# Channel mixing in 64-row products: one product per batch in place of one per pair of batches

## The reference, cut to what matters

```
agg_w = jnp.einsum('bk,koi->boi', att, weight[..., 0])
agg_b = att @ bias_k
y = jnp.einsum('boi,bih->boh', agg_w, x) + agg_b[:, :, None]
logits = y_flat @ W_router.T          # top 2 of 8, softmax over both
h = jnp.einsum('nd,erd->ner', y_flat, A)
expert_out = jnp.einsum('ner,eor->no', h * combine[:, :, None], B) * 2
out = x + y_flat @ W_base.T + b_base + expert_out
```

## Time and profile before

| what | value |
|---|---|
| device time, median of 3 runs | 1076.33 us (1075.97 to 1076.43) |
| span of the profiled execution | 1074.3 us |
| outside this span, up to the median | 2.0 us |
| instructions | 16995 |
| TensorE busy (matmul records) | 97% of the span |
| VectorE, ScalarE, GpSimd busy | 51%, 19%, 19% |

### The profile page before, as it was taken

One profiled execution on the slowest core, in us unless ns is written; L12 is line 12 of the kernel. 1 busy time (PEld: TensorE's weight loads), 2 busy tenths in 40 slices (PEclk: granted clock), 3 DMA queues, 4 the chain that ended last, 5 costly groups with the idle time before them and its releaser, 6 DMA issues.

```text
span 1074.3 us, 16995 instructions
## 1 busy us (share of the span) xinstructions
PE 1043.5 (97%) x6289; PEld 1037.5 (97%) x6289; DVE 543.5 (51%) x1298; ACT 201.2 (19%) x404; POOL 206.8 (19%) x138
## 2 busy tenths in 40 slices
PE   2799999999999999999999999999999999999998
PEld 1799999999999999999999999999999999999998
DVE  5854554554554554554554554554554554554551
ACT  5311211211211211211211211211211211211210
POOL 4621211211211211211211211211211211211210
PEclk9999999999999999999999999999999999999999
DMA  6621221221221221221221221221221221221200
GB/s 189 235 86 46 83 85 45 83 85 45 83 85 45 83 85 45 83 85 45 83 85 45 83 85 45 83 83 48 83 85 46 82 85 46 82 85 46 83 40 40
DMA packets 41836, 82.43 MB, mean 77 GB/s; under 512 B 13626, under 2 KB 24890, under 8 KB 41658
## 3 DMA queue, kind: packets, MB, share of 16 engines
q1 hardware_dynamic: 41826, 82.30, 23.9%
HBM read 46.46 MB, written 35.68 MB: 76 GB/s over the span
## 4 chain that ended last, share of the span: by engine, by line
PE 96%; DVE 2%; issue 1%; DMA 1%; ACT 0%; SPq 0%; DVEq 0%
PE ps_main L337 25%; PE ps_main L336 25%; PE ps_main L338 25%; PE ps_main L345 8%; PE ps_y L329 6%; PE ps_y L328 6%; DMA mix_space<-in_mix_w 1%; PE ps_main L409 1%; DVE y_parts L235 0%; PE ps_main L350 0%; DVE y_parts L579 0%; DMA mix<-mix_space 0%; DVE y_sb L569 0%; DVE mix_parts L558 0%; DVE y_sb L565 0%
## 5 line engine op out<-in xcount | busy, mean ns | idle before, releaser
L336 PE MATMUL ps_main<-w_hi,y_parts 128*128 128x388 f32 (+1 forms) x1536 | 526.0, 342 | 0.0
L337 PE MATMUL ps_main<-w_lo,y_parts 128*128 128x388 f32 (+1 forms) x1536 | 521.2, 339 | 0.0
L338 PE MATMUL ps_main<-w_hi,y_parts 128*128 128x388 f32 (+1 forms) x1536 | 520.1, 339 | 0.0
L336 PEld LDWEIGHTS ps_main<-w_hi,y_parts 128*128 128x128 f32 x1536 | 289.3, 188 | 2.3
L337 PEld LDWEIGHTS ps_main<-w_lo,y_parts 128*128 128x128 f32 x1536 | 289.7, 189 | 0.0
L338 PEld LDWEIGHTS ps_main<-w_hi,y_parts 128*128 128x128 f32 x1536 | 289.2, 188 | 0.0
L514 POOL TENSOR_TENSOR x_sb<-x_sb,bias_out 128x1024 f32<-128x1024 f32 x64 | 153.5, 2398 | 252.4 <-DVE x_lo L553 252.4
L436 ACT CAST y_parts<-y_sb 128x512 fp32r<-128x512 f32 x128 | 79.3, 620 | 378.6 <-DVE y_sb L569 378.6
L328 PE MATMUL ps_y<-mix_parts,x_hi 128*128 128x256 f32 x508 | 127.7, 283 | 10.9 <-DVE mix_parts L558 5.8
L510 POOL TENSOR_TENSOR mix_parts<-mix,mix_parts 128x128 fp32r<-128x128 f32 x62 | 28.7, 463 | 559.0 <-ACT mix_parts L432 559.0
L574 DVE TENSOR_TENSOR y_parts<-y_sb,y_parts 128x512 fp32r<-128x512 f32 x128 | 88.6, 692 | 87.8 <-ACT y_parts L436 87.7
(11 more groups left out here) (68 smaller groups left out, 470.3 us busy)
## 6 DMA issues: line engine op xcount, KB each, us to landing
x_sb<-in_x SPq DMA_DIRECT2D x64, 512.0 KB, 4.0
result<-x_sb SPq DMA_DIRECT2D x64, 512.0 KB, 2.7
bias_y<-agg_b_rows SPq DMA_DIRECT2D x64, 64.0 KB, 3.2
w_stage<-in_wide SPq DMA_DIRECT2D x4, 776.0 KB, 6.9
agg_w_rows<-mix_space SPq DMA_DIRECT2D x1, 2048.0 KB, 11.1
mix<-agg_w_rows SPq DMA_DIRECT2D x120, 16.0 KB, 2.2
w_stage<-in_wide SPq DMA_DIRECT2D x2, 768.0 KB, 11.6
mix_space<-in_mix_w SPq DMA_DIRECT2D x1, 650.0 KB
```

Source lines behind the costliest of these rows:

```text
L336: nc.tensor.matmul(dst, y_hi[:, u, cols], w_hi[:, c, piece], start=c == 0, stop=False)
L337: nc.tensor.matmul(dst, y_hi[:, u, cols], w_lo[:, c, piece], start=False, stop=False)
L338: return nc.tensor.matmul(dst, y_lo[:, u, cols], w_hi[:, c, piece], start=False, stop=c == DC - 1)
```

## The change

Each product over 128 stationary rows becomes two over 64 rows, one for each batch `b` of the pair. Rows 0 to 63 of `x_hi` meet the 64 columns of the first batch in the high part and the 64 in the low part of `mix_parts`, 128 moving columns in all; rows 64 to 127 meet those of the second batch. A call now issues 16 products with 16 weight loads. The products of the two batches are issued in turn (high part: batch 0, batch 1; low part: batch 0, batch 1). `ps_y` is laid out anew so that each batch has one of the two banks, and the two sums on VectorE read it in runs of 64 columns. Nothing else is changed; blank lines at the top of the file are gone, so that line numbers move by 16.

```
-        ps_y = ctx.enter_context(nc.psum_tensor("ps_y", [P, HC, 2, P], F32))
-        ps_y_flat = ps_y[:].rearrange("p c k n -> p (c k n)")
-        ps_y_first = ps_main[:, 1, 1:3, :].rearrange("p h (c k n) -> p (h c) k n", k=2, n=P)
+        ps_y = ctx.enter_context(nc.psum_tensor("ps_y", [P, PAIR, HC, 2, CH], F32))
+        ps_y_flat = ps_y[:].rearrange("p b c k o -> p (b c k o)")
+        ps_y_first = ps_main[:, 1, 1:3, :].rearrange("p b (c k o) -> p b c k o", k=2, o=CH)
...
                 for j in range(HC):
                     cols = slice((g * HC + j) * P, (g * HC + j + 1) * P)
-                    dst = into[:, j, :, :].rearrange("p k n -> p (k n)")
-                    nc.tensor.matmul(dst, x_hi[:, u, cols], mix_parts[:, u, :], start=True, stop=False)
-                    mm = nc.tensor.matmul(dst, x_lo[:, u, cols], mix_parts[:, u, :], start=False, stop=True)
+                    for part, first in ((x_hi, True), (x_lo, False)):
+                        for b in range(PAIR):
+                            rows = slice(b * CH, (b + 1) * CH)
+                            dst = into[:, b, j, :, :].rearrange("p k o -> p (k o)")
+                            own = mix_parts[rows, u, :].rearrange("p (k n) -> p k n", k=2)[:, :, rows]
+                            mm = nc.tensor.matmul(dst, part[rows, u, cols], own, start=first, stop=not first)
                 mm.then_inc(y_mm, 1)
...
             def y_sum(t, s, g, from_=ps_y):
 
-                half = y_sb[:, g * HD:(g + 1) * HD].rearrange("p (c n) -> p c n", c=HC)
+                half = y_sb[:, g * HD:(g + 1) * HD].rearrange("p (c b o) -> p c b o", c=HC, b=PAIR)
+                high, low = (from_[:, :, :, k, :].rearrange("p b c o -> p c b o") for k in range(2))
+                bias = bias_y[:, s, :].rearrange("p (b o) -> p b o", b=PAIR).unsqueeze(1)
                 dve.wait_ge(y_mm, halves(t, g))
-                nc.vector.tensor_tensor(half, from_[:, :, 0, :],
-                                        bias_y[:, s, :].unsqueeze(1).to_broadcast([P, HC, P]),
+                nc.vector.tensor_tensor(half, high, bias.to_broadcast([P, HC, PAIR, CH]),
                                         ALU.add).then_inc(y_part, 1)
                 dve.wait_ge(y_part, halves(t, g))
-                nc.vector.tensor_tensor(half, from_[:, :, 1, :], half, ALU.add).then_inc(y_summed, 1)
+                nc.vector.tensor_tensor(half, low, half, ALU.add).then_inc(y_summed, 1)
```

## The result

The changed kernel takes 1111.2 us (median of 4 runs, 1111.12 to 1111.36) against 1076.15 us: a ratio of 1.0326, 95% interval 1.0312 to 1.0341. It is slower by 35 us. I had forecast 1179 us. The measured time is close to that of the second rival (1110 us).

The account below looks back on a forecast made before the run. TensorE, busy 1043.5 of 1074.3 us, was taken as the bound; 125 calls at +0.81 us (+101) and the third call's +1.7 made +103 on 1076.3, so 1179 us, with row changes, sums and banks at nothing; range 1064 to 1212.

Parts of the forecast that it names:

- the second rival: Mixing on TensorE: both halves' loads side by side, but each 128/64-row change stops the array 0.17 us; 1110 us, chance 0.21.
- part (1): Mixing call: 16 loads one after another at 0.110 us, 1.76 us in place of 0.95; +101 us over 125 calls.
- the rule against the rows: Skill's rule that different tiles load and multiply in parallel, against traced load order; by it a small gain.
- the first rival: Mixing on TensorE: halves' loads side by side, row changes free; 0.88 us a call, -9 us, 1067 us, chance 0.27.
- Part (3): Array changing between 128 and 64 rows, 250 times on the path: forecast nothing; 0.17 us each, +43 us, for the range.
- Part (4): Two VectorE sums reading PSUM in runs of 64 columns, 0.68 and 0.69 us now: covered, cost 0.
- Part (5): PSUM banks of `ps_y`: two banks kept, each written until a call's end, nothing else reads them meanwhile; cost 0.
- part (2): Count of 128 mixing calls: first two hidden at start-up, third on the path +1.7 us, other 125 pay fully.

Follow-up runs that it names:

- the last run: Kernel before the change, low part of x multiplied by the mixing matrix's high part alone, 128 columns for 256 in every second product: 1073.1 us, ratio 0.9973.

## Why the prediction was wrong

The step that failed is part (1), "if the loads follow one another, each at the start of the product ahead as in the earlier trace rows". I read an order that holds for the same 128 rows as the order of all loads. In the changed kernel the second half's load starts within 0.01 us of the first's, ahead of a product that is still waiting. The section on the rule against the rows named this point: the Trainium skill (TensorEngine Tiling (Array Packing), Key Properties) says that tiles load and multiply in parallel, and here the traces agree, with 0.11 us for a pair of loads as for one. So a call costs 8 steps of a load and not 16: in place of the forecast's +101 us for part (1) the runs have -6 us (0.05 us in each of 125 calls). I weighted an observation that could not tell the cases apart over a rule that did.

The size of a load was right: 0.107 to 0.11 us for 128 float32r columns from the earlier trace rows, and the runs show 0.11 us in 64 rows and in 128. The run over all rows gave 1180.7 us where this price gives 1179. Because of it, the first rival's limit was right as well: side by side, a call's steps fall from 0.119 to 0.11 us and no further.

Part (3), the change of rows, I had set to nothing in the forecast and to 0.17 us in the second rival. It measured 0.20 us on the way in and 0.14 on the way out, 0.33 to 0.36 us for both in three runs (two changes fewer per tile, two more, and the table above). What stands in a stop can be read off the gaps between loads: the load for the other form comes when the columns of the last product are in and about 0.10 us more have passed, and then stands uncovered for 0.11 us. On the way in that is 506.49 + 0.16 + 0.10 = 506.75, the load in the row, and on the way out 507.64 + 0.05 + 0.10 = 507.79. The gaps behind a call of the wide and of the short pairs fit too (0.11 + 0.11 + 0.10 = 0.32, and 0.11 + 0.03 + 0.10 = 0.24 against 0.23). This is a reading of four gaps; the price of both changes does not hang on it. The same section of the Trainium skill says that changing the tiling mode drains the TensorE, and the runs show stops that fit a drain; the run with 96 rows shows that it goes with the form and not with any number of rows.

That the second rival's 1110 us came out within 2 us is in part luck. Its sum was -9 + 43; the runs give -6 for the pairs and 0.34 x 125 = +42 for the changes. But it had made its 0.17 us of another thing: a load that waits until the last product's record ends and is itself covered. In the rows above the load comes at 506.75, before that record ends (506.49 + 0.33 = 506.82), and is uncovered. And that rival's lower end of 1080 us does not follow from the bounds of part (3), whose lower bound of nothing gives 1067.

Part (4), VectorE's sums, was right: 681 and 692 ns on average after the change against 0.68 and 0.69 us, no wait of TensorE for them in the loop, and a cover that grew (from the end of the second sum to TensorE's next call 2.27 us before and 2.64 after, from 1076.67 to 1079.31). Part (5) holds. Of part (2) the count of 125 calls on the path holds, and the first two calls stay hidden; the 1.7 us for the third fell with part (1), since its loads ran in pairs as well. One reading of the earlier trace rows was low: lines 328 and 329 have 6% each, 12% and not 11%; no sum used it. The measured time lies inside the range and the direction was right. What was wrong is which case I held for the likeliest, and with it the size: 103 us forecast, 35 measured.

## What to carry to other kernels

Splitting products by rows pays here only if many of them stand between two changes: a pair saves 0.008 us (0.119 to 0.111), because each half still needs its own 0.11 us load, and every step into the 64-row form and back costs 0.34 us. By these numbers some 40 pairs would be needed between two changes (an estimate, 0.34 / 0.008), where this kernel has 8. Before products are made shorter, find out whether columns or weight loads pace them: halve the columns of some, as in the last run (3 us came back of 27), and see what comes back. And when a trace shows an order between operations on the same resource, do not carry it over to operations on separate ones.

## What the runs showed of the hardware that was not expected

- The halves of the array do not wait for the program's order. With batch 1's products behind batch 0's, four of each ran side by side.
- A lone half costs what two halves cost (1111.4 and 1111.2 us).
- The recorded start of a 64-row product does not keep step with its load. In the run with fewer columns the recorded starts of the pairs alternate by 0.08 and 0.14 us (511.23, 511.31, 511.45), while the loads step by 0.11. So I read the order of a call from the loads; where in this time the columns start is inferred, not measured.
